# Gains spread over the partitions by matmuls instead of by DRAM and broadcast DMAs

## The reference

```
mod = (silu(c) @ wmod).reshape(8, 6, 1, 128)
ga, gb = sign(g) * max(|g|, 0.25)
h = layernorm(x) * (1 + ca) + sa
x = x + ga * mix(h)          # block 0: state-space layer, then a norm with gamma, beta
h = layernorm(x) * (1 + cb) + sb
x = x + gb * ffn(h)          # block 0: four ternary layers; block 1: mixture of low-rank experts
```

## Time and profile before

| | |
|---|---|
| median of 3 runs | 545.56 us (545.25 to 547.88) |
| the profiled execution's own time | 545.56 us |
| its span, first to last instruction | 543.8 us |
| instructions | 9166 |
| DVE, ACT, POOL busy, share of the span | 75%, 60%, 35% |
| DMA | 32.72 MB, mean 60 GB/s |
| mean granted TensorE clock | 0.98 of full speed |

### The profile page before, as it was taken

The page is one execution under the profiler, slowest core; times in us unless marked ns, Lnnn a source line. Parts: engine busy times, 40 slices in busy tenths (PEclk is TensorE's granted clock), DMA queues, the critical chain, the costliest instruction groups (busy, mean ns, idle before and its releaser), DMA issues.

```text
span 543.8 us, 9166 instructions
## 1 busy us (share of the span) xinstructions
PE 504.6 (93%) x3257; PEld 386.2 (71%) x3257; DVE 408.8 (75%) x1019; ACT 323.6 (60%) x594; POOL 191.3 (35%) x245
## 2 busy tenths in 40 slices
PE   8599989998999999988998999999999979999994
PEld 7558767876787777765666667666676559888884
DVE  6986988697859774839898989898989864554433
ACT  4878868677876879653645444444445525556541
POOL 3511630133022002104437455564737553344311
PEclk9789999999999999998999999999999989999998
DMA  8500100000003002025323233333333000000101
GB/s 292 182 0 2 40 0 1 2 1 2 0 2 139 2 0 78 1 71 194 108 81 106 94 97 104 102 106 112 89 130 107 2 0 2 20 21 19 40 20 39
DMA packets 19230, 32.72 MB, mean 60 GB/s; under 512 B 2480, under 2 KB 13264, under 8 KB 19056
## 3 DMA queue, kind: packets, MB, share of 16 engines
q1 hardware_dynamic: 18128, 31.59, 17.9%
q10 hardware_dynamic: 1056, 0.52, 0.3%
HBM read 29.76 MB, written 2.34 MB: 59 GB/s over the span
## 4 chain that ended last, share of the span: by engine, by line
PE 47%; ACT 3%; DVE 2%; issue 2%; DMA 1%; POOL 0%; SPq 0%; DVEq 0%; ACTq 0%
PE bank L1937 10%; PE bank L2016 6%; PE bank L166 5%; PE bank L168 5%; PE bank L167 5%; PE bank L1949 3%; PE bank L1983 3%; PE bank L1971 2%; PE bank L242 2%; PE bank L1958 1%; PE bank L2008 1%; DMA att_prob<-cut_rows 1%; ACT att_qT L1774 1%; PE bank L2024 1%; PE bank L1961 1%
## 5 line engine op out<-in xcount | busy, mean ns | idle before, releaser
L1079 PE MATMUL bank<-ffn_g_hi,w_hi 128*128 128x512 f32 x288 | 116.4, 404 | 0.1
L1080 PE MATMUL bank<-ffn_g_lo,w_hi 128*128 128x512 f32 x288 | 114.0, 396 | 0.0
L1421 DVE TENSOR_TENSOR_SCAN att_prob<-att_prob,norm_out 128x512 f32<-128x512 f32 x64 | 97.1, 1521 | 5.6 <-DMA att_prob<-cut_rows 5.6
L617 DVE TENSOR_TENSOR ffn_g_lo<-ffn_full,ffn_g_hi 128x512 fp32r<-128x512 f32 x96 | 67.1, 699 | 26.6 <-ACT ffn_full L865 25.3
L1937 PE MATMUL bank<-att_qT,h_full 128*128 128x512 f32 x128 | 68.6, 620 | 0.0
L1079 PEld LDWEIGHTS bank<-ffn_g_hi,w_hi 128*128 128x128 f32 x288 | 54.3, 188 | 14.2 <-issue 1.7
L1801 ACT COPY att_qT<-bank 128x512 f32<-128x512 f32 x64 | 36.3, 585 | 45.5 <-PE bank L168 42.9
L1080 PEld LDWEIGHTS bank<-ffn_g_lo,w_hi 128*128 128x128 f32 x288 | 54.3, 189 | 12.0
L1613 POOL TENSOR_TENSOR att_vw<-att_v,att_prob 128x128 f32<-128x128 f32 x64 | 33.6, 531 | 68.9 <-DVE att_prob L1421 68.9
L865 ACT ACTIVATE ffn_full<-bank,cols 128x512 f32<-128x512 f32 x64 | 44.3, 699 | 20.9 <-PE bank L1080 18.1
L1432 DVE TENSOR_TENSOR att_prob<-bank,att_prob 128x512 f32<-128x512 f32 x64 | 42.8, 668 | 11.4 <-PE bank L1937 11.1
(11 more groups left out here) (232 smaller groups left out, 1153.2 us busy)
## 6 DMA issues: line engine op xcount, KB each, us to landing
att_prob<-cut_rows SPq DMA_DIRECT2D x32, 512.0 KB, 4.6
att_wide<-cum_rows SPq DMA_DIRECT2D x64, 48.0 KB, 1.9
out<-att_vw SPq DMA_DIRECT2D x7, 256.0 KB, 2.3
x<-in_x SPq DMA_DIRECT2D x3, 512.0 KB, 11.4
w_raw<-in_w_all SPq DMA_DIRECT2D x1, 1152.0 KB, 9.0
w_raw<-in_w_all SPq DMA_DIRECT2D x1, 768.0 KB, 9.9
v_raw<-in_v_all SPq DMA_DIRECT2D x1, 576.0 KB, 5.9
x<-in_x ACTq DMA_DIRECT2D x2, 256.0 KB, 3.1
```

The costliest lines, as they stand in the source:

```text
L617: dve.tensor_tensor(lo, full[j % 4][:, :], hi.bitcast(F32), ALU.subtract).then_inc(low, 1)
L1079: pe.matmul(acc, w[0], x[0], start=start, stop=False)
L1080: return pe.matmul(acc, w[0], x[1], start=False, stop=stop)
L1421: dve.tensor_tensor_scan(w, w, ident4[:, :], 0.0, ALU.mult, ALU.add).then_inc(decay_ready, 1)
```

## The change

The transpose, the DRAM tensor `gain_rows`, the SBUF tile `gains`, the copy at i = 0, j = 13, and the five DMAs of SP with their waits are taken out. In their place `spread` is called eight times instead of twice, through the list `SPREADS` of (table, half of the sequences): k = 0 and 1 in the set-up as before, k = 2 and 3 (tables 0 and 1, sequences 4 to 7) in pair 0 behind tiles 11 and 12 on PE and behind gelu 13 and 14 on ACT, k = 4 and 5 (table 2) in pair 3 behind tiles 11 and 12 on PE and 13 and 14 on ACT, and k = 6 and 7 (table 3) behind tiles 15 and 16 on PE and 17 and 18 on ACT. They use banks 6 and 7. POOL's `add_bias` waits for four spreads where b is at least 4; DVE's own wait there goes.

```diff
+    SPREAD = ("gain_attn0", "bias_attn0", "gain_attn1", "gain_ffn1")
+    SPREADS = [(0, 0), (1, 0), (0, 1), (1, 1), (2, 0), (2, 1), (3, 0), (3, 1)]
...
-                    if i == 0 and j == 11:
-                        uses.append((("turn", 0), 6))
+                    if i == 0 and j in (11, 12):
+                        uses.append((("spread", j - 9), 6 + j - 11))
...
+                    if i == 3 and j in (11, 12):
+                        uses.append((("spread", j - 7), 6 + j - 11))
+                    if i == 3 and j in (15, 16):
+                        uses.append((("spread", j - 9), 6 + j - 15))
...
-                rows_of = r["gain_rows"]
-                sp.wait_ge(turned, 1)
-                sp.dma_start(rows_of.rearrange("v b n -> (v b) n"), gains[:, :]).then_inc(gains_saved, 16)
-                sp.wait_ge(gains_saved, 16)
-                for v in range(2):
-                    sp.dma_start(r[SPREAD[v]][:, HALF:B, :], over(rows_of[v, HALF:B, :], 0, [P, B - HALF, D])).then_inc(gain_in, 16)
...
-                sp.wait_ge(mm, full_at("qk", 1))
-                for v, kept in enumerate((r["gain_attn1"], r["gain_ffn1"])):
-                    sp.dma_start(kept[:, :, :], over(rows_of[2 + v, :, :], 0, [P, B, D])).then_inc(gain_kept, 16)
-                sp.wait_ge(gain_kept, 32)
...
-                    if b >= HALF:
-                        dve.wait_ge(gain_in, 32)
...
-                    if b < HALF:
-                        pool.wait_ge(spread_ready, 2)
-                    else:
-                        pool.wait_ge(gain_in, 32)
+                    pool.wait_ge(spread_ready, 4 if b >= 4 else 2)
...
                 def spread(k):
+                    v, half = SPREADS[k]
                     act.wait_ge(mm, full_at("spread", k))
-                    dst = r[SPREAD[k]][:, 0:HALF, :].rearrange("p b n -> p (b n)")
+                    dst = r[SPREAD[v]][:, 4 * half:4 * half + 4, :].rearrange("p b n -> p (b n)")
                     act.copy(dst, bank("spread", k)[:, :]).then_inc(spread_ready, 1)
...
-                            if j == 13:
-                                act.wait_ge(mm, full_at("turn", 0))
-                                act.copy(gains[:, :], bank("turn", 0)[0:4 * B, 0:D]).then_inc(turned, 1)
+                            if j in (13, 14):
+                                spread(j - 11)
...
+                            if j in (13, 14):
+                                spread(j - 9)
...
+                            if j in (17, 18):
+                                spread(j - 11)
...
                 def spread(claim, k):
-                    pe.wait_ge(mod_ready, 4)
+                    v, half = SPREADS[k]
+                    pe.wait_ge(mod_ready, 8 if v >= 2 else 4)
                     ps = claim(pe, "spread", k)
-                    for q in range(HALF):
-                        col = spread_col[:, k, q:q + 1].broadcast_to([P, P])
+                    for q in range(4):
+                        col = spread_col[:, v, 4 * half + q:4 * half + q + 1].broadcast_to([P, P])
                         ins = pe.matmul(ps[:, q * P:(q + 1) * P], col, r["ident"][:, :], start=True, stop=True)
                     ins.then_inc(mm, 1)
-
-                def turn_gains(claim):
-                    pe.wait_ge(mod_ready, 8)
-                    ps = claim(pe, "turn", 0)
-                    pe.transpose(ps[0:4 * B, 0:D], spread_col[:, :, :].rearrange("p v b -> p (v b)"), r["ident"][:, :]).then_inc(mm, 1)
...
-                            if i == 0 and j == 11:
-                                turn_gains(claim)
+                            if i == 0 and j in (11, 12):
+                                spread(claim, j - 9)
...
+                                if j in (11, 12):
+                                    spread(claim, j - 7)
+                                if j in (15, 16):
+                                    spread(claim, j - 9)
```

More of the change, by code:

```diff
@@ L78, in build @@
         r["cum_rows"] = nc.dram_tensor("cum_rows", (B, NH, S - P), F32, kind="Internal").ap()
-        r["gain_rows"] = nc.dram_tensor("gain_rows", (4, B, D), F32, kind="Internal").ap()
         r["x"] = sb("x", [P, B, T, D])
@@ L261, in front @@
     STRIPS = 2 * SD
-    SPREAD = ("gain_attn0", "bias_attn0")
-    HALF = B // 2
+    SPREAD = ("gain_attn0", "bias_attn0", "gain_attn1", "gain_ffn1")
+    SPREADS = [(0, 0), (1, 0), (0, 1), (1, 1), (2, 0), (2, 1), (3, 0), (3, 1)]
     SOON = [(0, SA), (0, CA), (0, GA)]
@@ L283, in front @@
         gate_mag, gate_sgn, gate_col = sb("gate_mag", [P, 4 * B]), sb("gate_sgn", [P, 4 * B]), sb("gate_col", [P, 4 * B])
-        spread_col, gains = sb("spread_col", [P, 4, B]), sb("gains", [4 * B, D])
+        spread_col = sb("spread_col", [P, 4, B])
         sa_bo = sb("sa_bo", [P, B])
@@ L330, in front @@
         mod_ready, gate_step, col_ready, gap_ready, bias_ready = sem("mod_ready"), sem("gate_step"), sem("col_ready"), sem("gap_ready"), sem("bias_ready")
-        spread_ready, turned = sem("spread_ready"), sem("gains_turned")
-        gains_saved, gain_in, gain_kept = sem("gains_saved"), sem("gain_in"), sem("gain_kept")
+        spread_ready = sem("spread_ready")
         w_high, w_summed, w_flagged = sem("w_high"), sem("w_summed"), sem("w_flagged")
@@ L422, in __call__ @@
                         "gap": lambda k: (gap_ready, 1), "u": lambda p: (u_ready, p + 1), "z": lambda b: (znormed, b - 1) if b >= SLOTS else (centred, b + 1),
-                        "spread": lambda k: (spread_ready, k + 1), "turn": lambda k: (turned, 1), "flag": lambda k: (w_flagged, 1), "ffn": lambda b: (ffn_h_ready, b + 1),
+                        "spread": lambda k: (spread_ready, k + 1), "flag": lambda k: (w_flagged, 1), "ffn": lambda b: (ffn_h_ready, b + 1),
                         "gate": lambda i, j: (gate_ready, products(i, j)), "up": lambda i, j: (product_ready, products(i, j)),
```

## The result

The changed kernel takes 550.09 us (median of 20 runs, 546.92 to 552.4), the kernel before 546.85 us (20 runs, 545.05 to 549.16). The ratio of the two is 1.0052, with a 95% interval of 1.0034 to 1.0072: 2.8 us slower, 1.9 to 3.9 us. The two medians by themselves are 3.2 us apart. The prediction was 548.5 us and 2.94 us slower. Of the 1.6 us by which the time itself is higher, 1.3 us are the starting point, since the profiled run of before, 545.56 us, lies in the lower part of that kernel's own scatter.

The account below looks back on a forecast made before the run. PE (TensorE) was taken as the bound, with a later front end passed on whole. The profiled 545.56 us plus 0 (DMA), 0 (first pair) and 2.94 us (last pair) gave 548.5 us, range 546.3 to 550.4 us.

Parts of the forecast that it names:

- The DMA part: Removing five transfers and SP's waits: nothing waits for them, counted at 0, bounds 0 and a gain of 0.1 us.
- One spread: Four fp32 matmuls (eight instructions) added on PE: 0.90 us, taken from `keys`; bounds 0.44 and 1.02 us.
- The first pair: Two spreads behind tiles 11 and 12: PE's added 1.69 us go into 3.03 us of waits, cost 0.
- The last pair: Four spreads behind tiles 11, 12, 15, 16: 3.60 us less a 0.66 us wait, net 2.94 us.
- The starting point: Time of the kernel before, to which the terms were added: the profiled execution's 545.56 us.
- First pair not covered: Rival: in the first pair a dependence moves DVE along with PE, 1.69 us, 550.2 us; chance 0.08.
- ACT late: Rival: in the last pair two of ACT's copies reach PE, 1.1 us, 549.6 us; chance 0.05.
- a cheap spread: Rival: a spread costs less than `keys`, 0.67 us, giving 547.6 us; chance 0.06.
- The clock's rival: Half-clock fall near 253 us, priced 1.5 us: saved 547.0 us, chance 0.13; once more 550.0 us, chance 0.08.
- the flip of 76.39 us: Sign in the first pair: PE's flip waiting for ACT's ssm_out keeps its time; forecast wrong if it moves.
- the second flip of `early`: Sign in the last pair: PE's flip, at 211.56 us before, comes near 212.7 us without a wait.
- the front's last add: Sign at the front's end, before the barrier: this add, at 234.63 us before, starts near 237.6 us.

Follow-up runs that it names:

- e_none: Kernel before without the transpose, its copy, the five DMAs and the waits (output not the reference's): 546.36 us, ratio 0.9983 to before.
- e_diag: Changed kernel, each last-pair spread made as one 512-column fp32 matmul of ones with a diagonal tile built by POOL: 551.01 us, ratio 1.0071 to before.
- e_diag_r: Changed kernel, last-pair spreads made from POOL's diagonal split into high and low fp32r parts, two 512-column passes: 552.91 us, ratio 1.012 to before.
- e_first: Kernel before with only the first pair's half of the change, spreads 2 and 3 in pair 0: 546.61 us, ratio 0.9996 to before.
- e_triple_first: Changed kernel with each matmul of spreads 2 and 3 issued three times: 553.22 us, ratio 1.0102 to before.
- e_last: Kernel before with only the last pair's half of the change, four spreads in pair 3: 549.77 us, ratio 1.005 to before.
- e_double_last: Changed kernel with each matmul of the four last-pair spreads issued twice: 553.95 us, ratio 1.0132 to before.

## Why the prediction was right

- **The DMA part, 0.** Right for the front: `e_none`, with A to C of 156.59 us. For block 1 its timed runs, from 2.0 us faster to 0.2 us slower in all, don't decide.
- **One spread, 0.90 us.** Right in size: 0.90 us in the trace, 0.91 us from doubling. The choice of `keys` as the nearest row was right because it streams as many fp32 columns. That eight weight loads would also fit 0.90 us, as the prediction notes, is a coincidence as far as the runs tell: with two loads the same columns cost 0.86 us (`e_diag`), and as fp32r 0.45 us (`e_diag_r`). No run tries fewer columns with eight loads.
- **The first pair, 0.** Right: `e_first`, and 23.78 against 23.77 us. The order was as written: the first wait vanished, the rest went into the second. The cover was overrated, though, without harm: the prediction sets 1.69 us against 3.03 us of waits, and `e_triple_first` shows that about 2.6 us can be hidden, because beyond that DVE follows PE.
- **The last pair, 3.60 - 0.66 = 2.94 us.** Right: 2.88 us between A and C, of which 1.78 and 1.09 us on the two sides of the flip whose wait was used up. `e_last` has all of it, `e_double_last` shows that nothing else gives way.
- **The starting point.** The term that was off: I set the sum on one execution at 545.56 us; the kernel's median over 20 runs is 546.85 us.
- **Rivals.** "First pair not covered", "ACT late" and "a cheap spread" are excluded by `e_first`, `e_double_last` and the trace. The clock's rival described something real, but a property of single executions of both kernels, not of the change, and so part of the width of the range. One fall takes 1.7 us in the table, where the prediction priced 1.5 us.
- **The signs.** One was badly chosen: the forecast was to be wrong if the flip of 76.39 us moved. It did, to 77.40 us, but it stands between 76.39 and 77.76 us in the kernel before alone. The same 1.0 us stands in the other two: the second flip of `early` came at 213.71 us (212.7 expected), the front's last add at 238.52 us (237.6 expected). Only distances could decide, and they bear the prediction out.

## What to carry to other kernels

Price an added instruction by the stage it lands in: the same spread of eight PE instructions costs 0 us ahead of a wait of PE and 0.90 us in a full stretch. The waits behind the place are only the upper bound of what can be hidden; over-filling them shows where the engine that PE waits for begins to follow (here at 2.6 us, where the waits add up to 3.0). A transfer that nobody waits for costs nothing in this kernel, so replacing it with work on the engine that bounds the kernel can only lose. Where the effect is half a per cent, compare distances between landmarks inside the traces: they repeated to 0.1 us where whole runs scattered by 4 us.

## What the runs showed of the hardware that I had not expected

- An fp32 matmul pays for columns at half the rate: two passes of 512 columns cost 0.86 us, eight instructions of 128 columns 0.90 us, and two fp32r passes of 512 columns 0.45 us, at a granted clock of 1.00 throughout.
- Transfers of 1 MB landing beside full PE work, and their removal, changed none of the distances A to B and B to C by more than 0.1 us.
- DVE's operations took 1.6 to 3.6 times as long beside POOL's 128x512 products (a 128x512 cast 1.52 us instead of 0.42, a subtraction 1.41 instead of 0.69, h_full 1.83 instead of 1.11 us), so idle POOL time is not free where DVE is short.
- One kernel's executions on one core spread over 4 us (545.05 to 549.16 us), and its three traces lost 3.4 to 5.1 us of block 1 to the clock, at places that differ from one execution to the next (252 to 256 us in one, within 233 to 248 us in another).
